# The inverse roots of a graph layer's layer norm: one power operation on GpSimd for a seed and three Newton rounds

## What is computed

```python
def _layernorm(x, axis=-1, eps=1e-05):
    m = jnp.mean(x, axis=axis, keepdims=True)
    v = jnp.var(x, axis=axis, keepdims=True)
    return (x - m) / jnp.sqrt(v + eps)
...
h = jnp.maximum(_layernorm(x, axis=-1), 0.0)
msg_input = jnp.concatenate([h[src], h[dst]], axis=1)
for t in range(n_types):                       # 4
    m = jax.nn.relu(msg_input @ W1[t] + b1[t]) @ W2[t] + b2[t]
    msgs = msgs + jnp.where((edge_type == t)[:, None], m, 0)
agg = jax.ops.segment_sum(msgs, dst, num_segments=num_nodes)
gi, gh = agg @ W_ih.T + b_ih, h @ W_hh.T + b_hh
r = sigmoid(i_r + h_r); z = sigmoid(i_z + h_z); n = tanh(i_n + r * h_n)
return x + (1.0 - z) * n + z * h
```

## Time and profile before

| | |
|---|---|
| median of 3 runs | 1806.55 us (1804.4 to 1809.14) |
| the profiled execution | 1805.01 us |
| its span | 1803.1 us |
| TensorE busy | 1631.5 us (90%) |
| VectorE busy | 1592.3 us (88%) |
| ScalarE busy | 1460.1 us (81%) |
| GpSimd busy | 1235.9 us (69%) |
| the gathers of `e_x` on GpSimd | 852.5 us, 816 of them |
| lists written, on GpSimd | 95.4 us, 96 issues |
| the Newton rounds on GpSimd | 182.8 us, 624 operations |

### The profile page before, as it was taken

The page is one execution under the profiler, slowest core; times in us unless marked ns, Lnnn a source line. Parts: engine busy times, 40 slices in busy tenths (PEclk is TensorE's granted clock), DMA queues, the critical chain, the costliest instruction groups (busy, mean ns, idle before and its releaser), DMA issues.

```text
span 1803.1 us, 43100 instructions
## 1 busy us (share of the span) xinstructions
PE 1631.5 (90%) x10182; PEld 1428.9 (79%) x10182; DVE 1592.3 (88%) x4186; ACT 1460.1 (81%) x3401; POOL 1235.9 (69%) x1982
## 2 busy tenths in 40 slices
PE   0226799999999999999999999999999999999998
PEld 0115688888888888888888888888888888888887
DVE  8597699888989898898899999999999999999886
ACT  0025788888888888888888999989989999899895
POOL 4777777777777777777776676666767667676420
PEclk9985899999999999999999999999999999999999
DMA  2224677777777777777777777777777777777653
GB/s 70 50 46 125 166 191 194 195 188 192 193 195 193 194 197 188 188 188 191 193 190 196 195 195 199 193 197 197 196 198 194 199 199 192 200 193 197 182 145 96
DMA packets 477071, 319.72 MB, mean 177 GB/s; under 512 B 106705, under 2 KB 463009, under 8 KB 476962
## 3 DMA queue, kind: packets, MB, share of 16 engines
q10 hardware_dynamic: 261792, 156.12, 28.6%
q1 hardware_dynamic: 185730, 106.99, 25.9%
q0 software_dynamic: 29440, 55.47, 12.8%
HBM read 211.65 MB, written 106.72 MB: 177 GB/s over the span
## 4 chain that ended last, share of the span: by engine, by line
PE 77%; POOL 6%; issue 4%; DVE 2%; ACT 1%; POOLq 0%; ACTq 0%; DVEq 0%
PE bank L1332 14%; PE bank L1334 13%; PE bank L1333 13%; PE bank L1412 10%; PE bank L1424 4%; PE bank L1423 4%; PE bank L1440 4%; PE bank L1450 4%; PE bank L1402 4%; PE bank L1394 4%; POOL e_x L580 3%; DVE n_sel L1071 2%; PE bank L1436 1%; POOL lists L566 1%; ACT e_h L1177 0%
## 5 line engine op out<-in xcount | busy, mean ns | idle before, releaser
L580 POOL DMA_INDIRECT e_x<-in_x,rows_now x816 | 852.5, 1045 | 237.4 <-issue 220.5
L1177 ACT ACTIVATE e_h<-e_x,shift,rstd 128x128 f32<-128x128 f32 x816 | 355.4, 485 | 117.3 <-DVE shift L1048 93.3
L1194 ACT ACTIVATE n_h<-n_x,shift,rstd 128x128 f32<-128x128 f32 x784 | 385.0, 492 | 0.1
L1071 DVE TENSOR_SCALAR n_sel<-iota,n_rel 128x256 fp32r<-128x256 f32 x784 | 233.1, 359 | 37.6 <-POOL n_rel L631 35.7
L1412 PE MATMUL bank<-n_sel,n_win 128*128 128x256 f32 x1568 | 235.0, 292 | 31.0 <-DVE n_sel L1071 31.0
L1332 PE MATMUL bank<-n_h_hi,whh_hi 128*128 128x512 f32 x588 | 247.8, 421 | 2.9 <-ACT n_zc L1285 2.6
L1332 PE MATMUL bank<-n_a_hi,wih_hi 128*128 128x512 f32 x588 | 249.5, 424 | 0.9 <-DVE bank L1083 0.9
L1333 PE MATMUL bank<-n_h_lo,whh_hi 128*128 128x512 f32 x588 | 233.0, 396 | 0.0
L1334 PE MATMUL bank<-n_a_hi,wih_lo 128*128 128x512 f32 x588 | 232.6, 396 | 0.0
L1334 PE MATMUL bank<-n_h_hi,whh_lo 128*128 128x512 f32 x588 | 232.4, 395 | 0.0
L1333 PE MATMUL bank<-n_a_lo,wih_hi 128*128 128x512 f32 x588 | 232.1, 395 | 0.0
(11 more groups left out here) (179 smaller groups left out, 3757.7 us busy)
## 6 DMA issues: line engine op xcount, KB each, us to landing
n_win<-messages SPq DMA_DIRECT2D x1568, 64.2 KB
messages<-e_msg ACTq DMA_DIRECT2D x204, 257.0 KB, 3.1
n_x<-in_x ACTq DMA_DIRECT2D x195, 256.0 KB
out<-n_out ACTq DMA_DIRECT2D x195, 256.0 KB
e_x<-in_x,rows_now POOLq DMA_INDIRECT x816
rows_now<-lists SPq DMA_DIRECT2D x204, 2.0 KB, 3.0
lists<-picks,list_rows POOLq DMA_INDIRECT x72, 2.9
w<-in_W SPq DMA_DIRECT2D x1, 512.0 KB, 4.9
```

What stands on the lines that cost most here:

```text
L580: G.indirect_dma_start(e_x[:, s, 2 * end + t, :], None, x, bass.IndirectOffsetOnAxis(ap=rows_now[:, s, t, end:end + 1], axis=0)).then_inc( ...
L1071: ins = V.tensor_scalar(n_sel[:, s % 2, k, :], iota[:], n_rel[:, s % 2, k:k + 1], None, ALU.is_equal)
L1177: last = A.activation(e_h[:, s % 2, k, :], e_x[:, s, k, :], ACT.Relu, scale=rstd[:, slot, col + k:col + k + 1], bias=shift[:, slot, col + ...
L1194: last = A.activation(n_h[:, s % 2, cols], n_x[:, s, cols], ACT.Relu, scale=rstd[:, slot, col + 4 + k:col + 5 + k], bias=shift[:, slot, co ...
```

## The change

The three Newton rounds on GpSimd and the seed on VectorE go. In their place stands one operation on GpSimd, of the same 32 columns, that raises variance plus eps to the power of -0.5, which is given as a second operand of the same size. VectorE makes `var_eps` in the place of `half_var`. Six buffers become two, and two semaphores go.

```diff
@@ GpSimd, before the loops
-            G.memset(three_halves[:], 1.5)
+            G.memset(minus_half[:], -0.5)
@@ inverse_roots, at the end of GpSimd's steps with i % 4 == 1
-                made = [0]
-
-                def linked(ins, count=1):
-                    made[0] += count
-                    ins.then_inc(ln_ops, count)
-                    pool.wait_ge(ln_ops, first * (LN_ROOTS // 4) + made[0])
-
-                pool.wait_ge(ln_seeded, first + 4)
-                for old, new in ((root, root2), (root2, root), (root, None)):
-                    linked(G.tensor_tensor(root_t[:], old[:], old[:], ALU.mult))
-                    linked(G.tensor_tensor(root_u[:], root_t[:], half_var[:], ALU.mult))
-                    linked(G.tensor_tensor(root_t[:], three_halves[:], root_u[:], ALU.subtract), 1 if new is not None else 2)
-                    if new is not None:
-                        linked(G.tensor_tensor(new[:], root_t[:], old[:], ALU.mult))
+                pool.wait_ge(ln_vared, first + 4)
                 if due(first - 4):
                     pool.wait_ge(e_normed, first - 4)
                 if due(first - LAG + 5):
                     pool.wait_ge(n_normed, first - LAG + 5)
-                G.tensor_tensor(rstd[:, slot, :], root_t[:], root[:], ALU.mult).then_inc(ln_rooted, 4)
+                G.tensor_tensor(rstd[:, slot, :], var_eps[:], minus_half[:], ALU.pow).then_inc(ln_rooted, 4)
@@ ln_part, on VectorE
-                    V.tensor_scalar(half_var[:], bn[:, slot, :, 2], 0.5 / D, 0.5 * EPS, ALU.mult, ALU.add
+                    V.tensor_scalar(var_eps[:], bn[:, slot, :, 2], 1.0 / D, EPS, ALU.mult, ALU.add
                                     ).then_inc(ln_vared, 4)
-                elif (third, place) == (0, 7):
-                    dve.wait_ge(ln_vared, first + 4)
-                    V.tensor_scalar(root[:].bitcast(I32), half_var[:].bitcast(I32), -0.5, float(RSQRT_SEED - (1 << 22)),
-                                    ALU.mult, ALU.add).then_inc(ln_seeded, 4)
```

More of the change, by code:

```diff
@@ L175, in gnn_layer @@
         bn = sb("bn", [P, 2, LN_COLS, 3])
[L176 to L181, removed]
+        var_eps = sb("var_eps", [P, LN_COLS])
+        minus_half = sb("minus_half", [P, LN_COLS])
         rstd = sb("rstd", [P, 2, LN_COLS])
@@ L357, in gnn_layer @@
         ln_vared = sem("ln_vared")
-        ln_seeded = sem("ln_seeded")
-        ln_ops = sem("ln_ops")
         ln_rooted = sem("ln_rooted")
```

## The result

| | before | after |
|---|---|---|
| median | 1806.67 us (6 runs, 1804.4 to 1809.14) | 1823.22 us (6 runs, 1821.45 to 1824.32) |
| profiled execution | 1805.01 us, span 1803.1 | 1821.45 us, span 1819.6 |

The change makes the kernel slower: ratio 1.009, 95% interval 1.0077 to 1.0103, or 16.6 us. 1779 us was forecast.

A forecast was written before the change was run, and what follows sets the result against it. The prediction took TensorE as the bound, with GpSimd's chain stalling it early once in four steps. A 1.6 us power would end the stall: 1806.5 - 28 = 1779 us, range 1775 to 2005.

The forecast's parts named there:

- P: Time of one 128x32 power operation on GpSimd, taken as 1.6 us, with bounds of 0.25 and 11 us.
- What is added: On GpSimd, one power operation of 128x32 in place of the chain, costed at 1.6 us, with no new wait.
- The sum for a short root: Stall of TensorE removed: 1.18 us a group, 27.1 us over 23 groups, 28 with the single late stall.
- early stretch: 84 steps in which GpSimd also writes the lists: 698.67 us, TensorE idle 18.9 us, waiting for n_sel.
- late stretch: 84 steps without list writes on GpSimd: 674.85 us, bound by TensorE, which is idle 0.9 us.
- Below P = 2.9 the early stretch runs at the late one's pace: n_rel comes 4.37 - P earlier on GpSimd, and TensorE needs 1.45 us of that at most.
- Rival 1, the slow power: On GpSimd, a power above 4.4 us makes the kernel slower, 1866 us at P = 6; chance 0.36.
- the shared port: VectorE's n_xh might wait for the power; some 1.1 us is free, so it costs nothing at 1.6 us.
- Rival 2, VectorE held off: P of 3 to 4.4 us keeps the port and delays VectorE's n_xh: 1832 us at 4.0; chance 0.06.
- Rivals 3 and 4: 3: P of 3 to 4.4 us without port hold, 1803 us, chance 0.08; 4: windows' DMA keeps stall, 1806, 0.04.
- The step on what bounds the kernel: Late, TensorE bounds; early, it waits 18.6 us for n_sel, which waits for GpSimd's n_rel once in four steps.

The follow-up runs named there:

- 8 and 16 columns: Kernel after with the power over only the first 8 or 16 of 32 columns, the others keeping a 1: 1774.22 and 1774.47 us.
- newton_w15: Kernel before with GpSimd's list writes one step earlier, in steps 15 to 107 for 16 to 108: 1777.09 us (0.983).
- pow_late: Kernel before with Newton rounds in GpSimd's steps 0 to 111 and the power from 112 on: 1807.71 us (1.000).
- pow_split_from_20: Kernel after with the power in two halves, but one whole power for the four batches up to step 20: 1777.93 us (0.983).
- pow_split: Kernel after with the power in two halves of 16 columns, the second behind n_rel of the next step: 1783.17 us (0.987).
- pow_w15: Kernel after with GpSimd's list writes one step earlier, in steps 15 to 107 for 16 to 108: 1786.11 us (0.988).
- the probe: Kernel after with powers of 1 to 128 columns and products added behind GpSimd's last step; one execution, only the added operations' rows read.

## Why the prediction was wrong

**The size of P, in "What is added".** This is the step that failed and that turned the sign. I assumed 30 arithmetic passes of 0.047 us each for 32 columns, 1.6 us. The row says 5.47. In the same currency it is (5.47 - 0.2)/0.047 = 112 passes. The count was mine and rested on no row; the bounds, 0.25 and 11 us, held it. So the change lengthens GpSimd's work between the two gates by 1.1 us where I had it shorten by 2.8. How the power is worked out inside, and so why a column costs 158 ns, no run shows.

My estimate from the Trainium skill, "GPSIMD Engine Reference", "Performance pitfalls for Q7 kernels", 4 cycles for each step of a dependent fp32 chain, was 2.7 us for 25 assumed steps, and was low by half too.

**The sum for a short root** was right in mechanism, and short in size: 28 us forecast, 33 measured with 8 and 16 columns. The early stretch gives (698.67 - 673.45)/21 = 1.20 us a group where I had 1.18. The rest is where I had put nothing: 1.7 us in the late stretch (674.85 to 673.10), and 2 to 3 at the start (the first `n_sel` at 189.6 and 190.4 us with 8 and 16 columns, 192.6 before).

**"Below P = 2.9 the early stretch runs at the late one's pace"** was off: for a power it is 3.76. I took the time that the chain holds GpSimd, 4.37 us, as all that it costs. But what follows it moves too. The first gather behind the chain mostly starts after 0.40 us of idle time, and takes 1.47 to 1.49 us in 12 of the 21 early groups and 0.97 in 9; behind one power it starts after 0.17 us and takes 1.02. On the mean of the 21 groups that is 3.21 us from the gate to `n_rel` before and 2.67 after. What makes the long gathers long, and why the idle time is shorter, was not tried.

**Rival 1, the slow power**, is what happened, in the place that it names. Its decision point of 4.4 us was too low: by the early windows a power costs as much as the chain only at 4.96 us. Its formula gives 23 x 1.10 + 23 x 0.48 = 36 us for 5.47; 16.6 were measured. Early, it is 0.56 us a group (710.45 - 698.67 over 21) for 1.10, and the 0.54 that is missing is the shorter way from the gate to `n_rel`, 3.21 us to 2.67. Late, it is 0.08 to 0.18 (`pow_late` and the kernel after) for 0.48: I let the slack end at the start of `n_sel`. TensorE uses `n_sel` only some time later; the 0.35 us there stand in my own part on the shared port, and I left them out of the rival. Its slope of 1 us for each us of P holds between 4.21 and 5.47 us in the early windows ((710.45 - 682.99)/21 = 1.31 for 1.26), but not up to 10.94, where TensorE's clock adds to it.

**Rival 2, VectorE held off,** did not occur, neither with one power of 5.47 us nor with two in a row: `n_xh` starts inside the power and takes its 0.67 us. The Trainium skill's rule in "SBUF — State Buffer", "SBUF: two separate sides", of an exclusive lock for the whole instruction, is not what these rows show for a power.

**Rivals 3 and 4** did not occur: P is above 4.4 us, and with 8 and 16 columns the stall is gone. The step on what bounds the kernel was right, and `newton_w15` shows it without touching the roots.

**The chance and the range.** I gave slower 0.42, for a price that no row showed. The forecast should have given more weight to the distance between the two ends, 0.25 and 11 us, of which the break-even, 4.4 us, lay in the lower half. That 1823 us lies between 1775 and 2005 says little, since that range was made to hold a power of up to 9 us.

## What to carry to other kernels

Before an operation takes the place of a chain of cheap ones on an engine, measure it by itself at its size: the count of instructions (572 less here) says nothing if the one that is left costs 158 ns a column. When an engine is last only once in a few steps, look for what else stands between its two waits: moving three transfers by one step gained 30.7 us with the code of the roots untouched, and cutting the slow operation in two made the slower kernel faster than the one before. Count slack up to the engine that sets the end, not to the first one that waits.

Four versions that do all the work beat both kernels: `newton_w15` at 1777.09 us, `pow_split_from_20` at 1777.93, `pow_split` at 1783.17 and `pow_w15` at 1786.11. The floor in this arrangement is about 1774 us, that of the kernels with 8 and 16 columns, where TensorE has no idle time in the two stretches.

## What the runs showed of the hardware

- A power of two fp32 tensors on GpSimd takes 0.41 us and 0.158 us for each column (8, 16, 24 and 32 columns in the loop, 10.5 us for 64 and 20.8 for 128 in the probe), the same on 16 partitions as on 128. In the loop of the kernel after, one of 32 columns took 5433 to 5516 ns, 52 times.
- VectorE's operation with two inputs from SBUF ran at full pace, 0.67 to 0.69 us, inside 48 powers of 5.47 us, while a product of GpSimd that met the same operation was stretched from 0.25 to 0.79 us. The short operation waited for VectorE; the long one did not make VectorE wait.
- In the kernel with the power twice, TensorE's granted clock was 0.55 in the 3 us in which a wait of 5.4 us ended, and 0.57 and then 0.50 around the end of one of 7.0 us; the slower clock cost 1.4 to 2.4 us a group on top of the wait. With waits of up to 1.5 us it stayed at 1.00.
